# Packing the thirteenth key tile of the attention's gather over the rows

## The reference, cut to what matters

```python
q = (layernorm(x) @ Wq)                 # 64 rows, 16 heads of 64, for each of 32 batch entries
k, v = split(y @ Wkv)                   # 1601 keys
atten = softmax(q @ k.T * 64**-0.5)     # per head: 64 x 1601
x = x + concat(atten @ v) @ Wproj + bproj
```

## Time and profile before

| | |
|---|---|
| runs (median; lowest to highest) | 2605.01; 2601.64 to 2606.33 us |
| profiled execution: span, first to last instruction | 2605.3 us |
| busy: TensorE, weight loads | 2463.5 (95%), 1541.3 (59%) |
| busy: VectorE, ScalarE, GpSimd | 1761.7 (68%), 1201.7 (46%), 1798.6 (69%) |
| thirteenth tile, in 256 steps each | L570 with 65 rows and 384 columns, L571 with 65 rows and 192 columns |

### The profile page before, as it was taken

The page is one execution under the profiler, slowest core; times in us unless marked ns, Lnnn a source line. Parts: engine busy times, 40 slices in busy tenths (PEclk is TensorE's granted clock), DMA queues, the critical chain, the costliest instruction groups (busy, mean ns, idle before and its releaser), DMA issues. The chain is left out here.

```text
span 2605.3 us, 59585 instructions
## 1 busy us (share of the span) xinstructions
PE 2463.5 (95%) x23988; PEld 1541.3 (59%) x23988; DVE 1761.7 (68%) x3205; ACT 1201.7 (46%) x2037; POOL 1798.6 (69%) x1483
## 2 busy tenths in 40 slices
PE   5999999999999999999999999999987788899998
PEld 3666666666666666666666666666544122366665
DVE  5766666666666666666666666666666899766665
ACT  3343343344434334443434344343346788556665
POOL 5877777877777777777777777777511688565553
PEclk8999999999999999999999999999999899999999
DMA  7899989989999898999999999999840000021221
GB/s 207 178 183 184 185 180 174 194 173 187 179 187 179 177 193 171 187 179 185 182 188 183 177 189 178 183 183 188 172 99 1 21 1 1 14 74 55 60 59 43
DMA packets 1061619, 373.42 MB, mean 143 GB/s; under 512 B 983936, under 2 KB 1031680, under 8 KB 1061216
## 3 DMA queue, kind: packets, MB, share of 16 engines
q1 hardware_dynamic: 1061344, 369.61, 70.1%
HBM read 122.02 MB, written 4.19 MB: 48 GB/s over the span
## 5 line engine op out<-in xcount | busy, mean ns | idle before, releaser
L570 PE MATMUL psum<-yN,hT 128*128 128x384 f16 (+1 forms) x3328 | 838.2, 327 | 10.4 <-DMA lT<-xT 6.5
L571 PE MATMUL psum<-yN,lT 128*128 128x192 f16 (+1 forms) x3328 | 815.9, 246 | 0.0
L553 PE MATMUL psum<-yT,Q 128*128 128x512 f16 (+2 forms) x4096 | 744.8, 334 | 0.0
L553 PEld LDWEIGHTS psum<-yT,Q 128*128 128x128 f16 x4096 | 377.2, 97 | 374.3 <-issue 87.7
L509 POOL TENSOR_TENSOR pl<-prob,ph 128x1601 f16<-128x1601 f32 x128 | 414.3, 3237 | 222.5 <-DVE ph L852 222.5
L843 DVE TENSOR_REDUCE mx<-psum 128x1 f32<-128x801 f32 (+1 forms) x512 | 500.5, 988 | 88.9 <-PE psum L553 83.7
L509 POOL TENSOR_TENSOR xT<-xT 128x1601 f16<-128x1601 f32 x128 | 413.5, 3231 | 175.4 <-DVE xT L852 130.0
L570 PEld LDWEIGHTS psum<-yN,hT 128*128 128x128 f16 (+1 forms) x3328 | 325.7, 98 | 219.4 <-issue 13.6
L730 ACT ACTIVATE xT<-psum,nb 128x1601 f32<-128x1601 f32 x128 | 204.4, 1597 | 509.8 <-DVE nb L845 505.6
L730 ACT ACTIVATE prob<-psum,nb 128x1601 f32<-128x1601 f32 x128 | 204.4, 1597 | 508.6 <-DVE nb L845 504.4
L571 PEld LDWEIGHTS psum<-yN,lT 128*128 128x128 f16 (+1 forms) x3328 | 326.3, 98 | 6.2
(11 more groups left out here) (195 smaller groups left out, 3348.3 us busy)
## 6 DMA issues: line engine op xcount, KB each, us to landing
stage<-in_ctxN SPq DMA_DIRECT2D x96, 384.0 KB
wnat<-in_WF SPq DMA_DIRECT2D x31, 512.0 KB, 4.2
stage<-in_ctxT SPq DMA_DIRECT2D x32, 400.5 KB
stage<-in_ctxT SPq DMA_DIRECT2D x64, 200.2 KB
stage<-in_ctxT SPq DMA_DIRECT2D x32, 400.0 KB
stage<-in_ctxT SPq DMA_DIRECT2D x64, 200.0 KB
OT<-Oh SPq DMA_TRANSPOSE x256, 2.8
Q<-in_WkS SPq DMA_DIRECT2D x8, 256.0 KB, 7.6
```

Source lines behind the costliest of these rows:

```text
L553: ins = pe.matmul(psS[:, lo:hi], Q[p % 2][:, q, b, tt * P:(tt + 1) * P], yT[b][:, y, lo:hi], start=False, stop=(n == 3))
L570: pe.matmul(psO[:, 0:2 * CTX], hT[G % 2][0:k, n, :], yN[b][0:k, n, :], start=(n == 0), stop=False)
L571: ins = pe.matmul(psO[:, 0:CTX], lT[G % 2][0:k, n, :], yN[b][0:k, n, 0:CTX], start=False, stop=(n == JN - 1))
```

## The change

The thirteenth tile's 65 keys are taken as 64 keys and the last key.

- The 64 high probabilities are copied a second time behind themselves in `ph` (columns 1600 to 1663), so that their transposed tile has them in rows 0 to 63 and again in 64 to 127. The context tile has its high halves in rows 0 to 63 and its low halves in 64 to 127 of the first 192 columns. One product of 192 columns gives high times high and high times low.
- The last key's probability stands in `pl` as high, high, low (columns 1600 to 1602), beside the 64 low ones, and the last key's context in rows 64 to 66 of the other 192 columns as low, high, high.
- For that, VectorE makes two further copies behind the cast; GpSimd subtracts one more column in each step and cuts piece 7 with five operations; SP loads piece 7 with three transfers.

```diff
--- before.py
+++ after.py
@@ -28,6 +28,9 @@
 NPAIR = B // 2
 JT = J // P
 JR = J - JT * P
+JE = J - 1
+JB = JT * P
+HB = JE - JB
 JN = JT + 1
 C1 = CTX - P
 SCALE = DK ** -0.5
@@ -336,7 +339,7 @@
         biased = sem("biased")
         expd = sem("expd")
         recip = sem("recip")
-        hi_kept = sem("hi_kept")
+        hi_kept, hi_twice, odd_kept, tail_cut = sem("hi_kept"), sem("hi_twice"), sem("odd_kept"), sem("tail_cut")
         lo_kept = sem("lo_kept")
         hi_turned = [sem(f"hi_turned{i}") for i in range(2)]
         lo_turned = [sem(f"lo_turned{i}") for i in range(2)]
@@ -369,7 +372,7 @@
             return p, t, b, tt
 
         def transfers(part):
-            return 2 if part in (2, 3) else 1
+            return (1, 1, 2, 2, 1, 1, 1, 3)[part]
 
         def loaded_by(K):
 
@@ -399,7 +402,9 @@
                     m = 4 * (part - 4)
                     sp.dma_start(s[:, 0:4 * CTX].rearrange("p (m c) -> p m c", c=CTX), yn[:, m:m + 4, :]).then_inc(done, 16)
                 else:
-                    sp.dma_start(s[0:JR, 0:CTX], a["ctxR"][be]).then_inc(done, 16)
+                    for h in range(2):
+                        sp.dma_start(s[HB * h:HB * h + HB, 0:CTX], a["ctxR"][be][0:HB]).then_inc(done, 16)
+                    sp.dma_start(s[HB:HB + 3, CTX:2 * CTX], a["ctxR"][be][HB:JR].to_broadcast([3, CTX])).then_inc(done, 16)
 
             rows = a["x"].rearrange("(n p) c -> p n c", p=P)
             sp.dma_start(X[:, 0:2, :], rows[:, 0:2, :]).then_inc(x_in, 16)
@@ -422,7 +427,7 @@
             sp.dma_start(X[:, 2:, :], rows[:, 2:, :]).then_inc(x_rest, 16)
             for K in range(RING + 1, PIECES + 2):
                 load(K)
-            sp.wait_ge(pad_set, 4)
+            sp.wait_ge(pad_set, 2)
             def turn_o(G):
                 p, t, b, tt = place(G)
                 sp.wait_ge(o_kept, G + 1)
@@ -434,7 +439,7 @@
                 if G < NT:
                     if G >= 2:
                         sp.wait_ge(summed, G - 1)
-                    sp.wait_ge(hi_kept, G + 1)
+                    sp.wait_ge(hi_twice, G + 1)
                     sp.dma_start_transpose(hT[G % 2][:, :, :], ph[G % 2]).then_inc(hi_turned[G % 2], 16)
                 if G > BEHIND:
                     turn_o(G - BEHIND - 1)
@@ -476,12 +481,25 @@
                         pool.tensor_tensor(T_[low, 1, cols], v[low, :], T_[low, 1, cols], ALU.subtract).then_inc(piece_cut, 1)
                         if part == 2:
                             pool.wait_ge(piece_cut, K + 1)
+                elif part < 7:
+                    m = 4 * (part - 4)
+                    v = s[:, 0:4 * CTX].rearrange("p (m c) -> p m c", c=CTX)
+                    pool.tensor_copy(N_[:, m:m + 4, 0:CTX], v).then_inc(hi_cut, 1)
+                    pool.wait_ge(hi_cut, K + 1)
+                    pool.tensor_tensor(N_[:, m:m + 4, CTX:], v, N_[:, m:m + 4, 0:CTX], ALU.subtract).then_inc(piece_cut, 1)
                 else:
-                    m, w, r = 4 * (part - 4), (4, 4, 4, 1)[part - 4], JR if part == 7 else P
-                    v = s[0:r, 0:w * CTX].rearrange("p (m c) -> p m c", c=CTX)
-                    pool.tensor_copy(N_[0:r, m:m + w, 0:CTX], v).then_inc(hi_cut, 1)
+
+                    pool.tensor_copy(N_[:, JT, 0:CTX], s[:, 0:CTX]).then_inc(hi_cut, 1)
                     pool.wait_ge(hi_cut, K + 1)
-                    pool.tensor_tensor(N_[0:r, m:m + w, CTX:], v, N_[0:r, m:m + w, 0:CTX], ALU.subtract).then_inc(piece_cut, 1)
+                    pool.tensor_copy(N_[0:HB, JT, CTX:], s[0:HB, 0:CTX]).then_inc(tail_cut, 1)
+                    pool.wait_ge(tail_cut, 3 * be + 1)
+                    pool.tensor_copy(N_[HB:HB + 3, JT, CTX:], s[HB:HB + 3, CTX:2 * CTX]).then_inc(tail_cut, 1)
+                    pool.wait_ge(tail_cut, 3 * be + 2)
+                    pool.tensor_tensor(N_[HB:, JT, 0:CTX], s[HB:, 0:CTX], N_[HB:, JT, 0:CTX], ALU.subtract).then_inc(tail_cut, 1)
+                    pool.wait_ge(tail_cut, 3 * be + 3)
+                    pool.tensor_tensor(N_[HB:HB + 1, JT, CTX:], s[HB:HB + 1, CTX:2 * CTX], N_[HB:HB + 1, JT, CTX:],
+                                       ALU.subtract).then_inc(piece_cut, 1)
+                    pool.wait_ge(piece_cut, K + 1)
 
             pool.wait_ge(half_set, 1)
             def factor(norm, n, cols):
@@ -506,7 +524,9 @@
                 pool.wait_ge(hi_kept, G + 1)
                 if G >= 2:
                     pool.wait_ge(lo_turned[G % 2], 16 * (G // 2))
-                pool.tensor_tensor(pl[G % 2][:, 0:J], prob[G % 2], ph[G % 2][:, 0:J], ALU.subtract).then_inc(lo_kept, 1)
+                pool.tensor_tensor(pl[G % 2][:, 0:JE], prob[G % 2][:, 0:JE], ph[G % 2][:, 0:JE], ALU.subtract)
+                pool.wait_ge(odd_kept, G + 1)
+                pool.tensor_tensor(pl[G % 2][:, JE + 2:JE + 3], prob[G % 2][:, JE:J], pl[G % 2][:, JE:J], ALU.subtract).then_inc(lo_kept, 1)
                 if G + PIECES + 1 < B * PIECES:
                     cut(G + PIECES + 1)
             factor(ln2, 2, slice(NPAIR - 1, NPAIR))
@@ -565,11 +585,13 @@
                     pe.wait_ge(wvp_kept, 2 * CUTS)
                 pe.wait_ge(hi_turned[G % 2], 16 * (G // 2 + 1))
                 pe.wait_ge(lo_turned[G % 2], 16 * (G // 2 + 1))
-                for n in range(JN):
-                    k = P if n < JT else JR
-                    pe.matmul(psO[:, 0:2 * CTX], hT[G % 2][0:k, n, :], yN[b][0:k, n, :], start=(n == 0), stop=False)
-                    ins = pe.matmul(psO[:, 0:CTX], lT[G % 2][0:k, n, :], yN[b][0:k, n, 0:CTX], start=False, stop=(n == JN - 1))
-                ins.then_inc(summed, 1)
+                for n in range(JT):
+                    pe.matmul(psO[:, 0:2 * CTX], hT[G % 2][:, n, :], yN[b][:, n, :], start=(n == 0), stop=False)
+                    pe.matmul(psO[:, 0:CTX], lT[G % 2][:, n, :], yN[b][:, n, 0:CTX], start=False, stop=False)
+
+                pe.matmul(psO[:, 0:CTX], hT[G % 2][:, JT, :], yN[b][:, JT, 0:CTX], start=False, stop=False)
+                pe.matmul(psO[:, 0:CTX], lT[G % 2][0:HB + 3, JT, :], yN[b][0:HB + 3, JT, CTX:], start=False, stop=True)\
+                  .then_inc(summed, 1)
 
             def values(n):
                 p, half = divmod(n, 2)
@@ -849,7 +871,12 @@
                 dve.wait_ge(expd, G + 1)
                 if G >= 2:
                     dve.wait_ge(hi_turned[G % 2], 16 * (G // 2))
-                dve.tensor_copy(ph[G % 2][:, 0:J], prob[G % 2]).then_inc(hi_kept, 1)
+                dve.tensor_copy(ph[G % 2][:, 0:JE], prob[G % 2][:, 0:JE]).then_inc(hi_kept, 1)
+
+                dve.tensor_copy(ph[G % 2][:, JE:], prob[G % 2][:, JB:JE]).then_inc(hi_twice, 1)
+                if G >= 2:
+                    dve.wait_ge(lo_turned[G % 2], 16 * (G // 2))
+                dve.tensor_copy(pl[G % 2][:, JE:JE + 2], prob[G % 2][:, JE:J].to_broadcast([P, 2])).then_inc(odd_kept, 1)
 
             def reciprocal(G):
                 dve.wait_ge(expd, G + 1)
@@ -934,8 +961,8 @@
                 dve.tensor_tensor(folded(1, n), fold_bank(n), folded(0, n), ALU.subtract).then_inc(wvp_kept, 1)
 
             dve.memset(nhalf[:, :], -0.5).then_inc(half_set, 1)
-            for v in ph + pl:
-                dve.memset(v[:, J:], 0.0).then_inc(pad_set, 1)
+            for v in pl:
+                dve.memset(v[:, JE:], 0.0).then_inc(pad_set, 1)
             dve.wait_ge(x_in, 32)
             row_stats(range(2))
             factors(ln, slice(0, 2), 2)
```

## The result

The changed kernel takes 2634.88 us (median of 4 runs, 2622.70 to 2647.13) against 2603.33 for the one before beside it: 1.0123 times as long, 95% interval 1.0086 to 1.0161. The forecast was 2607, with 2586 to 2665 as its range. The profiled execution took 2643.76 us with a span of 2642.0, 36.7 more than the span of before.

The account below looks back on a forecast made before the run. TensorE was taken to set the pace, with a GpSimd-VectorE cycle of waits close behind. Shorter matmuls -21 us, waits at steps 9 to 14 +17, values at step 15 +6: +2, so 2607 us, range 2586 to 2665.

Parts of the forecast that it names:

- the sum: Forecast total over the profiled execution before (span 2605.3 us): -21 + 17 + 6 = +2, giving 2607 us.
- rival C: Step 8: bias addition after the cast makes the two-column copy wait for GpSimd's low halves; 3.5 us a pair, 2656; chance 0.16.
- TensorE, -0.082 a step: Thirteenth high product, 192 columns instead of 384: each of 256 steps 0.082 us shorter, -21.0 us; the only gain.
- VectorE's copies in the tolerance, 0.17: Two small copies between cast and reciprocal: 0.17 us a step, within the 0.59 us a cast may be late.
- the ring: GpSimd's low halves, next piece's cut, VectorE's cast, low halves again, each waiting: 6.65 to 6.77 us before, 6.78 to 6.90 changed.
- GpSimd's one column, +0.13: One more one-column subtraction on GpSimd in each step: 0.13 us longer from low halves to low halves (bounds 0.05 to 0.25).
- Thirteenth piece: Steps 6 and 14: GpSimd's cut of the thirteenth tile's piece in five operations, 2.55 us, +1.57 us.
- The ring's waits, +17 us at steps 9 to 14: Late casts make TensorE wait 1.2 us a pair over 14 pairs with both cuts and new queries: +17 us.
- Values at step 15, +6: Later casts delay the transposes the values wait for at step 15: +0.4 us a pair, +6 us.
- SP and DMA, nothing: Later transposes and two more small transfers every eighth load: hidden by SP's 136.4 us of waits in 90 steps.
- Rival B: Every step: two-column copy comes behind GpSimd's low halves and waits 3.23 us; VectorE becomes the bound, about 3270 us; chance 0.18.

Follow-up runs that it names:

- the bias moved: Changed kernel with GpSimd's bias addition at step 1 of each pair of 16 steps instead of step 8 (first pair excepted): 2606.3 us, 1.0007 times before.

## Why the prediction was right or wrong

The measured time lies 28 us above the forecast and inside its range. The profiled execution is 34.7 us longer than the sum has it, and rival C, which the forecast of 2607 left out, is 36.1 of that (35.0, and the 1.1 that the steps 9 should have gained). The terms one by one:

- *TensorE, -0.082 a step:* right: 6.84 and 6.40 for 6.91 and 6.47, and 17 us of it reach the end when nothing else is changed.
- *VectorE's copies in the tolerance, 0.17:* right in size (starts 0.10 and 0.07 apart); beside the low halves they cost the ring nothing. Put ahead of the cast they cost up to 1.19 us a pair.
- *GpSimd's one column, +0.13:* right: the ring's shortest laps went from 6.64 to 6.77.
- *Thirteenth piece:* 2.55 forecast, 2.39 measured (572.90 to 575.29).
- *The ring's waits, +17 us at steps 9 to 14:* over-sized. In the changed kernel steps 10 to 14 are together 2.1 us longer than before where the gain alone would have made them 5.7 shorter (5 x 14 x 0.082): some 8 us of waits. One reason is measured: I took the ring to be 6.90 at each transposed piece, working it out from the stretch with the bias addition, and 7.56 where that stands. With the bias moved the four laps are 6.87, 6.77, 6.83 and 6.88 (medians over 14 pairs), and in the changed kernel the lap with the bias addition is 7.34. That is 0.25 and 0.22 us a pair, up to 6 or 7 us in all.
- *Values at step 15, +6:* measured 4.1 + 1.1 = 5.2; the size was right in this execution, but part of the cause, the queue, was not in the sum.
- *SP and DMA, nothing:* this step failed. "SP waited 136.4 us in 90 steps" is true of the span and says nothing of t=13, where SP's round took 5.5 us of a 6.46 step before and 6.8 of a 6.40 step after (621.71 to 628.52). The transfers were priced as a total, not at the place where they stand. The price is small: TensorE's waits for the outputs' transposes grew by 2.9 us, from 5.2 to 8.1, and not all of that need be the queue.
- *The first pair* grew by 4.2 us, where the sum had -1.3; the cause stays open.
- *Rival C decided the result.* Its place, chain and price (3.5 a pair) were as written, as was its range for a part of the pairs, 2620 to 2650; 10 of 14 pairs give 35, and 2607 + 35 is the profiled run's span of 2642.0. That it fits so well is luck: without C the 14 pairs came out 8.6 us below the sum (-4.0 for +4.6) and the rest of the span 7.2 above it (+4.6 for -2.6). What failed is the weighing: C got 0.16 and no place in the 2607, though the earlier trace rows show the bias addition on either side of the cast. Before, it began 0.06 us ahead of the cast in 13 of the 14 pairs and behind it in one; in the changed kernel, where GpSimd's work ahead of it is longer, it began 0.16 us or more behind in all 14. There, and only there, VectorE's lead over the low halves is not 0.06 or more but nothing (0.01 behind).
- *Rival B* did not come: 0.06 of lead is enough, and in the ordinary steps of one run so was even -0.02.

On the rule of the Trainium skill that B and C drew on (SBUF — State Buffer, "Who interferes with whom": the one that starts first keeps the ports): the trace agrees where the copy starts 0.08 us or more behind the low halves, or 0.03 or more ahead of them. Between those the records don't tell who wins: 0.01 to 0.02 behind the low halves the copy passed in 176 of 176 steps in one kernel, and 0.01 behind it lost in 10 of 14 in the changed one. On what B took from Vector Engine (DVE) Microarchitecture Reference in the Trainium skill, section 5.1 (one repeated element, too, is copied in a two-port mode), the trace agrees: this copy, with one element as its source, is held up for 3.23 us.

The four runs of the changed kernel lie 24 us apart, those of the one with the bias moved 11. Pairs that toss at 3.0 to 3.9 us each would make such a spread; only one execution was profiled, so that it is they is argued, not shown.

## What to carry to other kernels

A short instruction that shares ports with a long one of another engine can cost nearly the long one's whole time (here 3.23 us for 0.16) if it starts just behind it, so look for the one step in the loop where something unusual (here a bias addition) puts the two at the same instant, and move that. Price the copies and transfers that a saving needs at the tightest step of each engine and queue, not against its idle time in the whole span. What sets the end can be the order in a DMA queue: send first what is needed first.

## What the runs showed of the hardware

Two neighbouring starts do not order two engines at the shared ports by their records alone: with the copy behind the reciprocal, VectorE's copy passed in the ordinary steps although its record starts 0.01 to 0.02 us later; at step 8, where VectorE's instruction before it had been held up, GpSimd won 10 of 14 at 0.01 in the changed kernel, and 14 of 14 at 0.08 to 0.09 with the copy behind the reciprocal. What decides between them below 0.08 us stays open. A copy of two columns takes 0.16 us alone and 3.23 when held. In the changed kernel a transfer of 2.2 KB takes SyncE's queue nearly as long as one of 48 KB: 0.47 and 0.59 us (medians).
